# A Mamba layer, attention and a mixture of experts on one core: causal mask moved from GpSimd to TensorE, first loads split over two queues, rows split five and three

## The reference, cut to what matters

```
x   = layernorm(X + (mamba2(X, ...) + X))                 # x1 of the kernel
q, k, v = split(x @ w_qkv)
scores  = where(causal, q @ k.T / sqrt(hd), lowest)       # causal mask
o   = (softmax(scores) @ v) @ w_o
h   = layernorm(x + o, g1, b1)
w   = top-2 of softmax(h @ wg), renormalised
y_e = gelu(h @ w1[e] + bb1[e]) @ w2[e] + bb2[e]           # per expert e
out = layernorm(x + layernorm(h + sum_e w_e y_e, g2, b2))
```

## Time and profile before

| | us |
|---|---|
| median of 3 runs (998.3 to 1010.81) | 1005.32 |
| the profiled execution | 1014.31 |
| its span, first to last instruction | 1012.6 |
| PE busy | 773.1 (76%) |
| DVE busy | 641.9 (63%) |
| ACT busy | 487.9 (48%) |
| POOL busy | 459.2 (45%) |

### The profile page before, as it was taken

The page is one execution under the profiler, slowest core; times in us unless marked ns, Lnnn a source line. Parts: engine busy times, 40 slices in busy tenths (PEclk is TensorE's granted clock), DMA queues, the critical chain, the costliest instruction groups (busy, mean ns, idle before and its releaser), DMA issues. The chain is left out here.

```text
span 1012.6 us, 18279 instructions
## 1 busy us (share of the span) xinstructions
PE 773.1 (76%) x5398; PEld 519.5 (51%) x5398; DVE 641.9 (63%) x1553; ACT 487.9 (48%) x1006; POOL 459.2 (45%) x595
## 2 busy tenths in 40 slices
PE   5879788887265365988899898999778887898720
PEld 3656565665243233444445454545325886898620
DVE  3788888987234473777767776858542564456653
ACT  3565555463145002656555555645635453454553
POOL 1333323333231011234553535444657788887773
PEclk9998988899677555999988999979968999999755
DMA  1000000000166531223442433220142222224422
GB/s 41 20 22 27 6 26 27 27 11 17 42 199 204 156 116 45 68 70 93 122 120 85 115 93 97 73 77 23 37 133 68 62 69 65 63 67 139 137 74 59
DMA packets 96846, 75.76 MB, mean 75 GB/s; under 512 B 15687, under 2 KB 87731, under 8 KB 96750
## 3 DMA queue, kind: packets, MB, share of 16 engines
q1 hardware_dynamic: 90990, 62.83, 22.6%
q0 software_dynamic: 5760, 11.77, 3.4%
HBM read 44.49 MB, written 25.25 MB: 69 GB/s over the span
## 5 line engine op out<-in xcount | busy, mean ns | idle before, releaser
L1618 ACT ACTIVATE pb<-psB 128x512 f32<-128x512 f32 (+1 forms) x352 | 191.9, 559 | 230.3 <-PE psB L2040 213.0
L1721 DVE TENSOR_REDUCE mx<-psB 128x1 f32<-128x384 f32 (+3 forms) x352 | 208.4, 634 | 91.7 <-PE psB L2022 82.2
L1570 POOL TENSOR_SCALAR_AFFINE_SELECT pb<-pb 128x512 f32<-128x512 f32 x128 | 81.1, 638 | 179.4 <-ACT pb L1618 177.2
L2020 PE MATMUL psB<-kx,qx 72*128 72x384 bf16 (+3 forms) x512 | 145.5, 335 | 21.4 <-DMA kx<-k_parts 19.6
L2040 PE MATMUL psB<-qx,kx 75*128 75x256 bf16 (+3 forms) x512 | 133.4, 322 | 33.5 <-DMA qx<-mparts 29.3
L2125 PE MATMUL psB<-hT_e,w1t 128*128 128x128 f32 x624 | 89.1, 288 | 30.0 <-ACT hT_e L1648 23.2
L2022 PE MATMUL psB<-hide,ident 128*128 128x128 bf16 x512 | 109.1, 238 | 0.0
L2055 PE MATMUL psB<-pb,vx 128*32 128x512 f32 (+3 forms) x1024 | 105.1, 487 | 2.8 <-POOL pb L1570 2.8
L2040 PEld LDWEIGHTS psB<-qx,kx 75*128 75x128 bf16 x512 | 46.1, 103 | 108.7 <-ACT pb L1618 52.4
L2125 PEld LDWEIGHTS psB<-hT_e,w1t 128*128 128x128 f32 x624 | 79.8, 200 | 34.7 <-ACT hT_e L1648 26.0
L2143 PE MATMUL psB<-w2s,gT 128*128 x624 | 88.2, 288 | 1.6 <-ACT gT L1653 1.6
(11 more groups left out here) (238 smaller groups left out, 1401.6 us busy)
## 6 DMA issues: line engine op xcount, KB each, us to landing
qx<-q_parts SPq DMA_DIRECT2D x96, 96.0 KB
kx<-k_parts SPq DMA_DIRECT2D x96, 96.0 KB
hin<-slots SPq DMA_DIRECT2D x78, 65.0 KB
ys<-results SPq DMA_DIRECT2D x16, 256.0 KB
q_parts<-qpart SPq DMA_DIRECT2D x8, 384.0 KB
k_parts<-kpart SPq DMA_DIRECT2D x8, 384.0 KB
xin<-in_L_attn_X SPq DMA_DIRECT2D x8, 256.0 KB
x_rows<-x1o SPq DMA_DIRECT2D x8, 256.0 KB
```

What stands on the lines that cost most here:

```text
L1570: nc.gpsimd.affine_select(out=pb[step % PBUF][:, :, 0:P], in_=pb[step % PBUF][:, :, 0:P], compare_op=ALU.is_ge, fill=0.0, base=0, pattern= ...
L1618: nc.scalar.activation(pb[step % PBUF][:, h0:h0 + heads, 0:width], src, ACT.Exp).then_inc(exp_ready, 2 if u == NEXP - 1 else 1)
L1721: nc.vector.tensor_reduce(mx[:, h0:h0 + heads, qt], ps[:, S_BANK + u % banks, 0:heads * width].rearrange("p (h n) -> p h n", n=width), AX. ...
L2020: nc.tensor.matmul(out, qx[q][0:QK_ROWS, h0 + j, qt * P:(qt + 1) * P], kx[q][0:QK_ROWS, h0 + j, 0:width], start=True, stop=False)
```

## The change

- **x1b moves to the Mamba stage.** POOL adds b2 to x1 of row b-1 after its third xw step of row b (`shift`), SP stores it after the next `move_c`. The projection stage loses the addition and the store, and the load of row b+2 waits only for PE's transposes of row b.
- **First loads on two queues.** q of row 0 stays on SP; k of row 0 and all 24 loads of row 1 are issued by ACT ahead of its first wait.
- **Causal mask on PE.** Each of the 64 exp matmuls a row is followed by a second one, 128 columns, that adds -3e38 above the diagonal (`hide` as weights, `ident16` moving). POOL's affine_select and the semaphore `masked` go; pv waits for the exponential itself.
- **w1 copies shared.** POOL copies w1 for even tiles, DVE for odd ones, each reads its own offsets from the table.
- **Fills by SP.** The 16 blocks of empty slots are plain 65 KB transfers with a register offset; those of part 0 are issued before the load of w1.
- **Five and three rows.** `SPLIT` = 5, parts of 47 and 31 tiles. `PLAN_ROW` stays row 7. The beats start one slot earlier, at 39.
- **Norm steps spread.** 14 beats instead of 9, statistics and their aggregation a beat apart, ACT's norms in halves, rows 0 to 4 start at beats 53, 57, 62, 66, 71, rows 5 to 7 at 82, 83, 84.

```diff
@@ mamba_layer, POOL
+            def shift(b):
+                if b == 0:
+                    pool.wait_ge(b2_loaded, 16)
+                pool.wait_ge(x1_ready, b + 1)
+                if b >= 2:
+                    pool.wait_ge(x1b_used[b % 2], 16 * (b // 2))
+                nc.gpsimd.tensor_tensor(x1b[b % 2][:, :, :], x1[b % 2][:, :, :], b2b[:, :].unsqueeze(1).broadcast_to([P, TILES, D]),
+                                        ALU.add).then_inc(x1b_ready, 1)
...
                 xw_step(row, 2)
+                if not first:
+                    shift(it * 2 + p - 1)
@@ mamba_layer, DVE, ahead of x1 (L624)
+                if it * 2 + p >= 2:
+                    dve.wait_ge(x1b_ready, it * 2 + p - 1)
@@ qkv_projection, POOL
-                    pool.wait_ge(x_loaded[p], (it + 1) * 16)
-                    if it:
-                        pool.wait_ge(shift_stored[p], it * 16)
-                    nc.gpsimd.tensor_tensor(x1b[p][:, :, :], x1[p][:, :, :], b2b[:, :].unsqueeze(1).broadcast_to([P, TILES, D]),
...
+                    pool.wait_ge(xT_ps, Row(it, p)(1, 1))
+                    load(pool, it, p + 2)
@@ tables
-SPLIT = 6
+SPLIT = 5
-FIRST_BEAT = -4
-EARLY_BEATS = {40: -4, 41: -3, 42: -2, 43: -1}
+FIRST_BEAT = -5
+EARLY_BEATS = {39: -5, 40: -4, 41: -3, 42: -2, 43: -1}
-NORM_AT = [FIRST_TILE[1] + 5 + 7 * b // 2 for b in range(SPLIT)] + [JOBS + 4 + i for i in range(BATCH - SPLIT)]
+NORM_AT = [FIRST_TILE[1] + 6 + 9 * b // 2 for b in range(SPLIT)] + [JOBS + 4 + i for i in range(BATCH - SPLIT)]
@@ w1 copies, used by POOL (even tiles) and DVE (odd tiles)
+        def copy_w1(eng, engine, j, at):
+
+            if j < 2:
+                eng.wait_ge(w1_loaded, E * 16)
+            wait(eng, up_ps, j - 3)
+            engine.tensor_copy(w1t[j % 4][:, :], w1s[:, bass.ds(at, F)]).then_inc(w1_ready[j % 2], 1)
@@ SP
+            def fill(g, e):
+
+                if e == 0:
+                    sp.wait_ge(planned[g], 2)
+                    if g == 0:
+                        sp.wait_ge(dead_filled, 32)
+                at = sp.value_load(fill_idx[g][0:1, e:e + 1], min_val=0, max_val=SLOTS - P)
+                sp.dma_start(slots[bass.ds(at, P), :], filler[:, :]).then_inc(filled[g], 16)
@@ ACT, start of the attention stage
+            for g in range(GROUPS):
+                for s in range(PARTS):
+                    load_k(act, 0, 0, g, s)
+            for g in range(GROUPS):
+                load_group(act, 0, 1, g)
             act.wait_ge(route_consts, CONSTS)
@@ PE, exp unit
-                    ins = nc.tensor.matmul(ps[:, E_BANK + u % E_BANKS, j * width:(j + 1) * width],
...
+                                           qx[q][0:MAX_ROWS, 4 * g + h0 + j, kt * P:SEQ], start=True, stop=False)
+                    ins = nc.tensor.matmul(out[:, 0:P], hide[:, :], ident16[:, :], start=False, stop=True)
@@ PE, pv
-                pe.wait_ge(masked, row(STEPS, step + 1))
+                pe.wait_ge(exp_ready, exps_done(row, LAST_UNIT[step]))
```

More of the change, by code:

```diff
@@ L158, in mamba_layer @@
         x1 = [sb(f"x1o{p}", [P, TILES, D]) for p in range(2)]
+        x1b = [sb(f"x1bo{p}", [P, TILES, D]) for p in range(2)]
+        b2b = sb("b2_a", [P, D])
         ps = ctx.enter_context(nc.psum_tensor("psA", [P, 8, 512], F32))
@@ L336, in _ @@
             norm(Row(BATCH // 2 - 1, 1))
+            shift(BATCH - 1)
         @block.scalar
@@ L881, in qkv_projection @@
         v = pair("v_b", [P, TILES, D])
-        b2b = sb("b2_b", [P, D])
-        x1b = pair("x1b_b", [P, TILES, D])
         ps = ctx.enter_context(nc.psum_tensor("psB0", [P, 8, 512], F32))
@@ L1031 @@
 EXP_COUNT = NEXP + 1
+LAST_UNIT = {g * TILES + kt: u for u, (g, kt, _, _) in enumerate(EXP_UNITS)}
 PBUF = 4
@@ L1067, in schedule @@
     out, done = [], 0
-    last_unit = {g * TILES + kt: u for u, (g, kt, _, _) in enumerate(EXP_UNITS)}
+    last_unit = LAST_UNIT
     for slot in range(NEXP):
@@ L1081, in schedule @@
             out += [("plan", i) for i, at in enumerate(PLAN_AT) if at == slot]
-            out += [("fill", e) for e, at in enumerate(FILL_AT) if at == slot]
         if b == BATCH - 1 and slot in EARLY_BEATS:
@@ L1092, in after @@
     out = []
-    for beat in range(AFTER_BEAT, max(NORM_AT) + 10):
+    for beat in range(AFTER_BEAT, max(NORM_AT) + 15):
         if beat < JOBS + 4:
@@ L1413, in _ @@
             sp.wait_ge(e_ps, (BATCH - 1) * NEXP)
+            for e in range(E):
+                fill(0, e)
             sp.wait_ge(s_ps, (BATCH - 1) * NMAX)
@@ L1424, in _ @@
                     copy_h(sp, end, 1)
+                elif what == "fill" and row == BATCH:
+                    fill(1, n)
                 elif what == "load norm":
@@ L1563, in body @@
                 for what, n in items:
-                    if what == "exp":
-                        g, kt, h0, heads = EXP_UNITS[n]
-                        if h0 + heads == 4:
-                            step = g * TILES + kt
-                            wait_apart(pool, exp_ready, exps_done(row, n), pool_passed)
-                            nc.gpsimd.affine_select(out=pb[step % PBUF][:, :, 0:P], in_=pb[step % PBUF][:, :, 0:P],
-                                                    compare_op=ALU.is_ge, fill=0.0, base=0,
-                                                    pattern=[[0, 4], [1, P]], channel_multiplier=-1).then_inc(masked, 1)
-                    elif what == "spread v" and not last:
+                    if what == "spread v" and not last:
                         if not first:
```

156 lines of the change are left out of this document (74 added, 82 removed).

## The result

The changed kernel takes 971.97 us (median of 4 runs, 971.19 to 975.48), the kernel before 1003.73 us (4 runs, 998.3 to 1010.81). The ratio is 0.9686, with a 95% interval of 0.9619 to 0.9753: faster by 32 us. The prediction said 989, faster by 16 us against the 1005 it had. The time lies inside its range, the size of the gain does not agree.

The account below looks back on a forecast made before the run. It took PE to bound the attention rows, and a load, compute, store chain the projection. Terms +2 - 16 - 12 + 26 - 9 - 1 - 11 + 5 = -16 on the 1005.3 us median gave 989, range 970 to 1010.

Parts of the forecast that it names:

- Projection, -16: Projection stage: without x1b's store, loads prefetch two rows ahead and DMA becomes the bound, -16 us.
- Start of attention, -12: Start of attention: maxima no longer queue behind row 1's loads, -13; first loads +1; sum -12 us.
- Masks on PE, +26: Attention rows: 512 mask matmuls cost 33 us on a bound PE, less absorbed waits, leaving +26 us.
- Row 7, +3: Last attention row, not PE-bound throughout: its 64 mask matmuls take 5 us, of which 3 counted within the masks' 33.
- rival A: Attention rows: PE's gaps swallow most of the masks or denser PE keeps its clock, +8 not +26, 971 us; chance 0.17.
- Fills, -9: Experts' beats: eight fills leave POOL, so their beats fall from 3.06 to 1.88 us, -9 us.
- Sharing w1, -1: Experts' first scatter beats: POOL keeps half the w1 copies, DVE takes the others, -1 us.
- Norms, -11: Experts' beats 53 to 79: five rows of norms spread out, 65 us instead of 76, -11 us.
- Third row, +5: End of the kernel: a third row of norms left there, 5 us a row and its loads beside it, +5 us.
- B: Experts' beats: DVE's w1 copies and POOL block each other, 37 us on top, 1026 us; chance 0.08.
- C: Start of attention: the maxima still wait because ACT's loads fill the DMA engines, gain 0, 1001 us; chance 0.10.
- D: Last beats: norms cost what they did and the third row adds 5 us, 1000 us; chance 0.15.

Follow-up runs that it names:

- e7: Changed kernel with the addition of b2 and the store of x1b back in the projection stage: 988.3 us.
- e5: Changed kernel with all 48 first loads of attention back on SP in the old order: 976.1 us.
- e6: Changed kernel with q and k of row 0 on SP in pairs and only row 1's 24 loads on ACT: 988.2 us.
- e1: Changed kernel with the causal masks of the exponentials put back on POOL: 967.8 us.
- e2: Kernel before with only the masks moved from POOL to PE: 1005.4 us.
- e14: Kernel before without any causal mask on the exponentials: 990.6 us.
- e3: Changed kernel without any causal mask on the exponentials: 959.7 us.
- e4: Changed kernel with every mask matmul of the exponentials issued twice, at half the constant each: 992.2 us.
- e11: Changed kernel with all 78 w1 copies, and their table reads, on POOL: 974.5 us.
- e12: Changed kernel with the 16 fills as POOL's indirect transfers again: 980.3 us.
- e9: Changed kernel with the dense norm steps of the kernel before, five and three rows and their starts kept: 993.1 us.
- e10: Changed kernel with parts of six and two rows again, norm steps still spread: 968.3 us.

## Why the prediction was right or wrong

**Mamba, +2.** The projection's first transpose came 0.5 us later. In the profiles of all runs it comes between 275.3 and 280.1 us, so a term of 2 us cannot be told from none.

**Projection, -16.** e7 gives -16. The size was right, the reason half: the two waits behind x1b's store, 8.1 and 8.3 us, went in full, where I had counted on losing half of that again and on DMA as the new bound for the rest. Of the seven steps from row to row four are 3.05 us, less than the 4.1 that I had as the bound of DMA, and the DMA share of the stage (268 to 319.6 us, the 69 us of before now 51.6) is 0.69, not over 0.8.

**Start of attention, -12.** Measured -6.7 (e5) and -7.5 (table). The mechanism was right. Two sizes were off: the first group came 3 us later than before instead of 1, and the transfer of the maxima took 7.0 us to the exp, not 4. Row 1's loads were still running on ACT's queue then, and e6, where they had landed, has 3.6.

**Masks on PE, +26.** This is the step that failed. Measured: +4 in both kernels (e1, e2). The full row grew from 45.27 to 45.97 us, 0.7, where the prediction itself named under 1.5 us as a sign of being wrong. The term (its own parts, 33 - 5 - 2.8, give 25, not 26) had two errors, and each can be read in the sum. First, "Of the 33 us, some fall where PE waited for the maxima ... -5": I took PE as the bound because it was busy 298 of 326 us, so that nothing else could absorb. A set costs 15 us by e14 and e2, not 33 - 5 = 28; a third of its busy time goes into PE's idle time in every row, which is split over many waits for exponentials, maxima and copies. The series e3, changed, e4 shows how this slack runs out. The same windows give 3.1 us of busy time for a set where I had 3.8. Of the waits for the maxima the set took 3.3 us (7.6 in e14, 4.3 in e2), not 5. Second, "The wait for POOL's masks, -2.8, goes too": the select cost 11 us. Only 2.8 of it stood under its own name, all in row 7; in the full rows it stood as longer waits under other names, for the maxima, for DVE and under "issue" at L2063 (e14). 15 - 11 = 4.

**Row 7, +3.** The table's -4.1 for the rows has row 7 6 us shorter. That is not the masks' doing as far as the runs show. With the masks on PE, row 7 took 54.5 (e5), 55.0 (e11), 56.2 (changed), 59.1 (e7) and 62.0 us (e6) at granted clocks of 0.94, 0.91, 0.88, 0.83 and 0.78; the kernel before had 61.9 at 0.78. What sets the clock there stays open. In rows 1 to 6 the mean clock was 0.98 or 0.99 in nine of ten profiles with masks on PE, and 0.95 to 0.99 in the six without them, so part of rival A (a denser PE keeps its clock) may be true, but it is not shown.

**Fills, -9.** e12: -8 by the medians, -6.8 by the stretch; the beats there take 35.8 / 16 = 2.2 us, not 1.9. **Sharing w1, -1.** e11: 0 by the stretches, -2.5 by the medians, neither clear of the scatter; the 3 to 5 us lost in the first beats, where DVE has work of its own, I had not looked for.

**Norms, -11.** The stretch from tile 57 to the last down matmul is 10.9 us shorter. I had taken the new starts and the spacing as one; it is the spread steps that do it (e9: 75.1 us without them), not five and three rows (e10: 53.2 us with six and two). I had said that ACT's waits for the shift would be gone; they are shorter, 6.2 and 1.5 us.

**Third row, +5.** The end is 4.5 us longer, but the number agrees by luck. With two rows at the end and spread steps it is 47.1 us (e10), with three rows and dense steps 45.6 (e9), with both edits 46.2, against 41.7 before. So with spread steps the end is as long with two rows as with three. The prediction had the cost of the spread steps there at nothing, and beside them the third row adds nothing.

Rival A, masks nearly free at 971 us, came closest in time, with "+8 instead of +26". B did not come (a median of 0.42 us for DVE's copies, with two long ones), C too (the maxima waited 8.2 instead of 18.5 us), and D by the 10.9 us.

The terms sum to -16, the medians differ by 32. With 4 in place of 26 and 7 in place of 12 the sum is -33. That it agrees to 1 us is closer than these measures allow: the ratio alone is known to 7 us either way.

## What to carry to other kernels

An engine that is busy 91% of a stretch by its modelled ends can still swallow a third of what is added to it; find its price by adding the work twice and leaving it out, since the steps between the three tell slack from bound. A stage that feeds an engine can cost more than the wait that carries its name: compare all waits of that engine with and without it, those put down as "issue" too. When an order is made of many stages, space the steps so that no in-order engine holds its queue on a fresh result, and try each size of the new plan (here the split) without the others.
